# A six-stage decoder kernel: time-step chain in two halves, block-step rows, and the last steps of silu and gate on GpSimd

## The chip, the cores and the metric

The kernel runs on one core of a Trainium2 chip. The metric is the device time of one execution in microseconds (us). Five engines matter: TensorE (PE in the profile), VectorE (DVE), ScalarE (ACT), GpSimd (POOL) and SyncE (SP), which here only issues DMAs.

## The reference, cut to what matters

The reference runs six blocks over x of 4 x 256 tokens by 256 features, each with a layer norm in front and a residual behind. The kernel names them stages A to F: attention (A), hard-routed experts (B), a mixture of experts (C), a state-space block (D), attention without projections (E), a second mixture of experts (F). The change is in D and in the second half of C. D computes, with 64 heads of width 8, chunks of 128 tokens and 8 groups of state size 64:

```python
xBCzA = jnp.einsum('bld,ed->ble', input_, in_proj_w)
xBC, z, A_log = ...                       # 1536, 512 and 64 columns
xBC = silu(causal depthwise conv of 4 taps(xBC) + bias)
x, Bm, Cm = ...                           # 512, 512 and 512 columns
dt = jax.nn.softplus(A_log)
A_cum = jnp.cumsum(-dt within the chunk)
Lm = jnp.exp(segsum(A))                   # lower triangle: exp(A_cum[s] - A_cum[z]), above it 0
Y_diag = jnp.einsum('bcshn,bczhn,bhcsz,bczhp->bcshp', Cm, Bm, Lm, X)
states = jnp.einsum('bcshn,bhcs,bcshp->bchpn', Bm, exp(A_cum[-1] - A_cum), X)
Y_off = jnp.einsum('bcshn,bchpn,bhcs->bcshp', Cm, states before, exp(A_cum))
yf = Y_diag + Y_off + D * x / dt
out = jnp.einsum('bld,ed->ble', yf * jax.nn.silu(z + z_bias), out_proj_w)
```

## The kernel before, in words

`schedule` writes one list of steps (kind, stage, index) for the whole kernel, and every engine walks the same list and does its share of each step, so the list is the order of work on every engine. Semaphores carry the data dependences. PSUM banks are rings; `number` gives each use its place. Ring T is one bank, with a wait of PE for the read of the use before it.

**Stage C.** It goes over the tokens in two halves. A half has 13 tiles of hidden units (2 shared, 11 routed). For a tile j PE does 12 matmuls of 512 columns (L1374), ACT the silu, DVE two products (L1746, L1751), ACT and DVE split the result in two parts (L973, L1757), and PE multiplies tile j - 2 by the down weights (L1398). ACT and POOL split the weights of tile j + 2 (L961, L791). Beside the second half stand the first 8 channel pairs of D (`BESIDE_C`): projection on PE (din, din2: L1411, L1418), a copy to SBUF on ACT (ev: L996, L998), three conv taps on DVE (L1781), silu on ACT (L1007).

**Stage D before its loop.** When C has ended, DVE adds the residual (L1704) and normalises batches 2 and 3 (L1544 to L1555, with the power on POOL, L739). PE turns them (lt: L1168). Then comes the time-step chain for all 8 x 64 columns at once: projection (dt_in: L1433), a softplus that POOL, ACT and DVE hand to one another (L1013 to L1029, L817 to L827, L1807 to L1810), cumulative sums by a triangular matmul (acum: L1441), copies (L1033), a split in three bf16 parts (L1824 to L1833), a transpose for unit 0 (at: L1446), its copy (atc: L1044, L1045), and SP's DMAs that put the rows in the form that the loop wants (L711, L713). Channel pair 8 stands between.

**The loop of D.** Its 8 units are the (batch, chunk) pairs. A unit has 16 slots (`NHG`), one for each 4 heads; `LAG` and `MUL_LAG` say how many slots later the scan and the mul of a slot stand, and `UNIT_SLOTS` and `PAIR_SLOTS` the slots of all else. In a slot:

- ssd: PE writes a bank with a mask (a matmul of `maskt` with the identity, 0 or -1e30: L1482) and adds the differences of cumulative sums, a matmul with 15 contraction rows (L1484);
- exp: ACT writes exp of the bank to one of 8 buffers M (L1066);
- mul: DVE multiplies M by the C-B product in place (L1849), both inputs in SBUF;
- scan: PE multiplies with the spread x (L1136), after `m_ready`.

Around them, in a unit: the C-B products (cb: PE L1469, copied by DVE in cbc: L1839), the chunk states (L1494, L1504, yo: L1858), the projection and gate of z (dz, dz2, zt: L1798, zth on ACT: L1019, zsm: L1801), y_t, yfs (DVE: Du added L1875, Y_off added in odd units L1880, times the gate L1881), the output projection (L1512 to L1521, added to x by dx, L1885), xt and xtp (transposed x, spread and multiplied by POOL: L843 to L852). Three channel pairs stand beside each of units 0 to 4: L1411, L1418, L996, L998, the taps L1781, th (tanh) on ACT L1009 and silu on DVE L1791. `raw` has two buffers: ev of a pair waits for the silu of the pair two before it (`xs_ready`). The input of ring R (L1411) waits for the read of the use before.

The lines of the loop as they stand before:

```python
("ssd")  mm(bk[:, :], identb[:, :], maskt[:, :].unsqueeze(1).to_broadcast([P, HG, P]),
            start=True, stop=False, skip_group_check=True)
         mm(bk[:, :], rows_z[:, hg, :], rows_s[:, :, hg, :], start=False, stop=True,
            skip_group_check=True).then_inc(e_full, 1)
("mul")  v.tensor_tensor(m, m, CBs[:, u % 2, hg // (NV // NG):NG:NG // HG, :], ALU.mult).then_inc(m_ready, 1)
```

## Time and profile before

| | us |
|---|---|
| median of 3 runs | 995.91 (994.95 to 996.75) |
| the profiled execution: its time | 990.7 |
| its span | 988.9 |
| end of C's last matmul to the first ssd of D | 408.68 to 455.65 |
| loop of D (first cb to the last matmuls) | 456.7 to about 700 |

| engine | busy | of the span |
|---|---|---|
| PE | 810.5 | 82% |
| DVE | 577.0 | 58% |
| ACT | 383.7 | 39% |
| POOL | 216.6 | 22% |

The shares are means over six stages with different limits. The page's slices show PE at nine tenths and more from about 460 to 680 us, with DVE at seven to eight tenths, and both low around 420 to 450 us. The granted TensorE clock had a mean of 0.899 over the span.

### The profile page before, as it was taken

The page shows a single profiled execution, that of the slowest core. Times are in us where ns is not written, and L with a number is a line of the kernel's source. Part 1 is how long each engine was busy: PE and PEld are TensorE (multiplying, and loading weights), DVE is VectorE, ACT ScalarE, POOL GpSimd, SP SyncE. Part 2 cuts the span into 40 slices and gives each one's busy share as a digit, 9 for nine tenths or more (in the row PEclk, how much of TensorE's full clock was granted, in tenths as well). Part 3 has the DMA queues.
Part 4 walks back from the last instruction along what each step waited for, and adds up shares of the span by engine and source line. Part 5 has one row for each costly group of instructions (what it writes and reads, how often), then busy time and mean ns, then how long its engine had stood idle before and what let it go on. Part 6 is the DMA issues. An engine that isn't in the chain of part 4 may idle for free.

```text
span 988.9 us, 14763 instructions
## 1 busy us (share of the span) xinstructions
PE 810.5 (82%) x5680; PEld 523.6 (53%) x5680; DVE 577.0 (58%) x1188; ACT 383.7 (39%) x653; POOL 216.6 (22%) x210
## 2 busy tenths in 40 slices
PE   1577777599799799656999999998667786899998
PEld 0334443258677588533445444444445454677776
DVE  5666642544545457525878788568566653545443
ACT  1124334101444355233566465354124344444442
POOL 3200000223433322141101111011411201442432
PEclk9889979799999899866989899699778788899999
DMA  9000001001121211000000000000000001222331
GB/s 311 29 2 1 3 1 49 1 0 32 49 81 53 71 54 33 9 0 5 5 3 6 4 5 6 3 5 4 1 2 2 1 1 50 81 80 64 84 96 40
DMA packets 17831, 32.77 MB, mean 33 GB/s; under 512 B 5819, under 2 KB 9787, under 8 KB 17494
## 3 DMA queue, kind: packets, MB, share of 16 engines
q1 hardware_dynamic: 17762, 31.83, 10.4%
q8 instruction: 46, 0.75, 0.3%
q14 instruction: 23, 0.19, 0.1%
HBM read 29.85 MB, written 1.05 MB: 31 GB/s over the span
## 4 chain that ended last, share of the span: by engine, by line
PE 60%; DVE 20%; issue 9%; ACT 4%; POOL 4%; DMA 1%; SPq 1%; DVEq 0%; ACTq 0%; POOLq 0%
PE bank L1374 13%; PE bank L1398 8%; PE bank L1136 4%; PE bank L1484 3%; PE bank L1321 3%; PE bank L1482 3%; PE bank L1411 3%; PE bank L1418 2%; DVE s_xn L1555 2%; PE bank L1336 2%; DVE s_arena L1627 2%; PE bank L1265 2%; POOL s_rstd L739 1%; PE bank L1208 1%; PE bank L1384 1%
## 5 line engine op out<-in xcount | busy, mean ns | idle before, releaser
L791 POOL TENSOR_TENSOR s_wl<-s_wmoe,s_wh 128x768 fp32r<-128x768 f32 x54 | 99.2, 1839 | 175.0 <-ACT s_wh L961 175.0
L910 ACT ACTIVATE s_arena<-bank 128x512 f32<-128x512 f32 x96 | 56.6, 597 | 106.2 <-PE bank L1241 55.2
L1746 DVE TENSOR_TENSOR s_act<-bank,s_sg_moe 128x512 f32<-128x512 f32 x54 | 37.3, 691 | 82.4 <-PE bank L1374 75.8
L1627 DVE TENSOR_REDUCE s_arena<-bank 128x2 f32<-128x512 f32 (+1 forms) x96 | 64.6, 686 | 35.6 <-PE bank L1212 18.9
L1374 PE MATMUL bank<-s_xh,s_wh 128*128 128x512 f32 x216 | 73.1, 421 | 8.2 <-POOL s_wl L791 8.2
L973 ACT CAST s_ah<-s_act 128x512 fp32r<-128x512 f32 x54 | 33.6, 621 | 101.7 <-DVE s_act L1751 79.2
L1374 PE MATMUL bank<-s_xl,s_wh 128*128 128x512 f32 x216 | 69.3, 403 | 0.0
L1398 PE MATMUL bank<-s_wh,s_ah 128*128 128x256 f32 x216 | 66.5, 308 | 2.8 <-DVE s_al L1757 2.8
L1374 PE MATMUL bank<-s_xh,s_wl 128*128 128x512 f32 x216 | 68.4, 399 | 0.0
L1781 DVE SCALAR_TENSOR_TENSOR s_arena<-s_arena,s_convw 128x256 f32<-128x256 f32 x144 | 63.7, 483 | 0.6
L1398 PE MATMUL bank<-s_wl,s_ah 128*128 128x256 f32 x216 | 61.6, 285 | 0.0
L1398 PE MATMUL bank<-s_wh,s_al 128*128 128x256 f32 x216 | 61.5, 285 | 0.0
L1757 DVE TENSOR_TENSOR s_al<-s_act,s_ah 128x512 fp32r<-128x512 f32 x54 | 37.3, 691 | 40.3 <-ACT s_ah L973 40.2
L1066 ACT ACTIVATE s_arena<-bank 128x512 f32<-128x512 f32 x64 | 38.2, 597 | 50.1 <-PE bank L1484 50.1
L1482 PE MATMUL bank<-s_maskt,s_identb 128*128 128x512 bf16 x128 | 52.3, 408 | 5.1 <-DMA s_arena<-s_arena 4.3
L739 POOL TENSOR_TENSOR s_rstd<-s_ve,s_mhalf 128x2 f32<-128x2 f32 x24 | 16.6, 691 | 175.0 <-DVE s_ve L1547 174.7
L1849 DVE TENSOR_TENSOR s_arena<-s_arena 128x512 f32<-128x512 f32 x64 | 42.9, 685 | 15.9 <-ACT s_arena L1066 15.6
L1484 PE MATMUL bank<-s_arena 15*128 15x512 bf16 x128 | 51.9, 406 | 0.0
L1066 ACT ACTIVATE s_early<-bank 128x512 f32<-128x512 f32 x64 | 38.4, 601 | 30.2 <-PE bank L1484 29.9
L1398 PEld LDWEIGHTS bank<-s_wh,s_ah 128*128 128x128 f32 x216 | 41.4, 192 | 13.5 <-issue 8.2
L1374 PEld LDWEIGHTS bank<-s_xl,s_wh 128*128 128x128 f32 x216 | 42.5, 197 | 9.8
L1168 PE MATMUL bank<-s_ident,s_xn 128*128 128x128 f32 x80 | 15.5, 327 | 39.0 <-DVE s_xn L1555 36.9
(232 smaller groups left out, 1745.6 us busy)
## 6 DMA issues: line engine op xcount, KB each, us to landing
s_wmoe<-in_wF SPq DMA_DIRECT2D x28, 384.0 KB, 3.1
s_wmoe<-in_wC SPq DMA_DIRECT2D x26, 384.0 KB, 3.0
s_win<-in_win SPq DMA_DIRECT2D x1, 2112.0 KB, 10.4
s_x<-in_x SPq DMA_DIRECT2D x4, 256.0 KB, 3.5
s_early<-in_ctxT SPq DMA_DIRECT2D x1, 1024.0 KB, 9.5
s_ctxn<-in_ctx SPq DMA_DIRECT2D x1, 1024.0 KB, 12.3
s_arena<-s_arena SPq DMA_DIRECT2D x64, 6.0 KB
out_x<-s_x SPq DMA_DIRECT2D x4, 256.0 KB, 2.8
```

Of the source, the lines that this page charges most:

```text
L791: g.tensor_tensor(wl[:, w % NS_, :], wmoe[:, w % NW, :], wh[:, w % NS_, :], ALU.subtract).then_inc(wl_ready, 1)
L910: a.activation(PT[:, p % NPT, :], AR[n % 3][:, :], ACT.Exp).then_inc(a_read, 1)
L1066: a.activation(M[k % NM], S[k % 2][:, :], ACT.Exp).then_inc(e_read, 1)
L1136: ins = mm(bk[j * 32:(j + 1) * 32, quarter * P:(quarter + 1) * P], xsp[u % 2][:, quarter, h, j, :, :].rearrange("p q w -> p (q w)"), M[k % ...
L1374: ins = mm(G[2 * (n % 2) + half][:, :], a_[:, k, half, :], b_[:, k, toks], start=(p_ == 0), stop=(p_ == len(parts) - 1))
L1398: ins = mm(Y[t // NT][:, (t % NT) * D:(t % NT + 1) * D], a_[:, w % NA, t * P:(t + 1) * P], b_[:, w % NS_, 2 * KD * P:], start=(j == 0 and ...
L1482: mm(bk[:, :], identb[:, :], maskt[:, :].unsqueeze(1).to_broadcast([P, HG, P]), start=True, stop=False, skip_group_check=True)
L1484: mm(bk[:, :], rows_z[:, hg, :], rows_s[:, :, hg, :], start=False, stop=True, skip_group_check=True).then_inc(e_full, 1)
L1627: v.tensor_reduce(nM[:, q, h0:h0 + heads], V[n % 2][:, :].rearrange("p (h k) -> p h k", h=heads), AX.X, ALU.max, negate=True).then_inc(v_r ...
L1746: v.tensor_tensor(act_[:, w % 2, :], G[2 * (n % 2) + 1][:, :], sg_moe[:, n % 2, :], ALU.mult).then_inc(g_read, 1)
L1781: ins = v.scalar_tensor_tensor(o, raw[:, m % NRAW, h, KS - 1 - k:KS - 1 - k + L], convw[:, ct, KS - 1 - k:KS - k], o, ALU.mult, ALU.add)
L1849: v.tensor_tensor(m, m, CBs[:, u % 2, hg // (NV // NG):NG:NG // HG, :], ALU.mult).then_inc(m_ready, 1)
```

## The change

Five things change.

1. The time-step chain is cut in two halves of 4 units (256 columns). Its steps have names of their own (dt_in, dtc, dt_p1 to dt_p3, dt_a1 to dt_a3, dt_sum, acum, acumc, last, lastc, dec_in, dec_exp, ap_hi, ap_mid, ap_lo, ddt). The first half stands beside tiles 4 to 10 of C's second half (`BESIDE_C_STEPS`), the second in slots 21 to 44 of D's loop (`SECOND_STEPS`: units 1 and 2). The turns of batches 2 and 3 move into slots 2 and 3 of the loop (`LATER_TURNS`). Its scratch moves from the M buffers, yf and yo to the part of `early` that is free by then. The POOL memsets of the spread buffers stand in xtp of units 0 and 1.
2. The mask is no matmul any more. 15 further contraction rows (`blocks` times steps in `onehot`, 16 columns a block) put -1e30 above the blocks on the diagonal; within a block the entries above the diagonal stay, mul clamps them with `min 1.0`, and cbc multiplies the C-B product by the lower triangle, both as `scalar_tensor_tensor` on DVE. `onehot` grows from 12 to 27 rows of 16 KB, and one DMA (`blocks`, 15 rows of 4 KB) is new.
3. silu of D's pairs goes from one DVE instruction to two `tensor_tensor` on POOL (L840, L841 of the kernel after). The same for the gate of z, zsm (L844, L845).
4. yfs keeps its first add on DVE; the add of Y_off and the product with the gate become the POOL step yfp (L850, L852), in slot 8.
5. The first pair of the loop is number 8 instead of 9, and some slots move by one.

The diff, cut to its core (the bodies of the renamed chain steps are as before, over 256 columns instead of 512, and are left out):

```diff
-FIRST_PAIRS = 9
+FIRST_PAIRS = 8
...
-UNIT_SLOTS = ((0, "cb", 0), (3, "state", 0), (3, "at", 1), (6, "y_t", -1), (7, "dz", 1), (8, "dz2", 1), (9, "dy_t", -1),
-              (12, "dy", -1), (13, "dy2", -1), (14, "xt", 1), (15, "xt1", 1),
-              (4, "atc", 1), (5, "ysc", -1), (7, "stc", 0), (10, "yfc", -1), (11, "zth", 1), (15, "xtc", 1), (15, "xtp", 1),
+UNIT_SLOTS = ((0, "cb", 0), (3, "state", 0), (3, "at", 1), (6, "y_t", -1), (7, "dz", 1), (8, "dz2", 1), (10, "dy_t", -1),
+              (13, "dy", -1), (14, "dy2", -1), (14, "xt", 1), (15, "xt1", 1),
+              (4, "atc", 1), (5, "ysc", -1), (7, "stc", 0), (11, "yfc", -1), (11, "zth", 1), (15, "xtc", 1), (15, "xtp", 1),
               (16, "xt1c", 1),
-              (1, "cbc", 0), (4, "yo", 0), (7, "yfs", -1), (9, "zt", 1), (12, "zsm", 1), (14, "dx", -1))
+              (1, "cbc", 0), (4, "yo", 0), (7, "yfs", -1), (8, "yfp", -1), (9, "zt", 1), (12, "zsm", 1), (15, "dx", -1))
+LATER_TURNS = (2, 3)
+SECOND_STEPS = ((21, "dt_in"), (22, "dtc"), (23, "dt_p1"), (24, "dt_a1"), (25, "dt_p2"), (26, "dt_a2"), (27, "dt_p3"), (28, "dt_a3"),
+                (29, "dt_sum"), (33, "acum"), (34, "acumc"), (37, "last"), (38, "lastc"), (39, "dec_in"), (40, "dec_exp"),
+                (41, "ap_hi"), (42, "ap_mid"), (43, "ap_lo"), (44, "ddt"))
+BESIDE_C_STEPS = ((4, "dt_in"), (4, "dtc"), (4, "dt_p1"), (5, "dt_a1"), (5, "dt_p2"), (5, "dt_a2"), (6, "dt_p3"), (6, "dt_a3"),
+                  (6, "dt_sum"), (7, "acum"), (7, "acumc"), (8, "last"), (8, "lastc"), (8, "dec_in"), (9, "dec_exp"),
+                  (9, "ap_hi"), (9, "ap_mid"), (10, "ap_lo"), (10, "ddt"))
 PAIR_SLOTS = (((1, "din"), (2, "din2"), (3, "ev"), (5, 1), (6, 2), (8, 3), (9, "th"), (10, "silu")),
               ((4, "din"), (5, "din2"), (6, "ev"), (9, 1), (10, 2), (11, 3), (12, "th"), (13, "silu")),
               ((10, "din"), (11, "din2"), (12, "ev"), (13, 1), (14, 2), (15, 3), (16, "th"), (18, "silu")))
-RR = 3 + 3 * HG
+RL = 3 + 3 * HG
+STEPS = 16
+RR = RL + STEPS - 1
...
+                        steps.extend((kind, nxt, 0) for at_j, kind in BESIDE_C_STEPS if at_j == j)
...
-            if not beside_c:
-                steps.append(("d_init", s, 0))
-            while late:
-                turn(*late.pop(0))
-            steps.append(("dt_in", s, 0))
-            chain = ["dt", "acum", "at", "atc", "ddt"]
-            for m in range(beside_c, FIRST_PAIRS):
-                din(m)
-                if m > beside_c:
-                    silu(m - 1)
-                if m == beside_c:
-                    steps.extend((kind, s, 0) for kind in ("dz", "dz2", "zt"))
-                taps(m)
-                if chain:
-                    steps.append((chain.pop(0), s, 0))
-            silu(FIRST_PAIRS - 1)
-            steps.extend((kind, s, 0) for kind in chain)
-            steps.extend((kind, s, 0) for kind in ("zth", "zsm", "xt", "xtc", "xtp", "xt1", "xt1c"))
+            assert beside_c == FIRST_PAIRS
+            steps.extend((kind, s, 0) for kind in ("at", "atc", "xt", "xtc", "xtp", "xt1", "xt1c", "dz", "dz2", "zt", "zth", "zsm"))
             units = B * NT
             slots = {}
 
             def put(slot, kind, key):
                 slots.setdefault(slot, []).append((kind, s, key))
 
+            for slot, (stage, b) in zip(LATER_TURNS, late):
+                put(slot, "lt", b)
+            late.clear()
+            for slot, kind in SECOND_STEPS:
+                put(slot, kind, 1)
...
+                    sp.dma_start(rows_z[RL:RR, :, :], A["blocks"]).then_inc(hot_in, 16)
...
+                elif kind == "silu":
+                    b, j = i
+                    m = b * (CT // 2) + j
+                    if m < beside_c:
+                        continue
+                    pool.wait_ge(tanh_ready, m - beside_c + 1)
+                    half, th = xs[:, b % 2, 2 * j:2 * j + 2, :], raw[:, m % NRAW, :, KS - 1:]
+                    link(g.tensor_tensor(th, th, half, ALU.mult))
+                    g.tensor_tensor(half, th, half, ALU.add).then_inc(xs_ready, 1)
+                elif kind == "zsm":
+                    pool.wait_ge(z_tanh, i + 1)
+                    link(g.tensor_tensor(zs[:, i % 2, :], zs[:, i % 2, :], zt[:, :], ALU.mult))
+                    g.tensor_tensor(zs[:, i % 2, :], zs[:, i % 2, :], zt[:, :], ALU.add).then_inc(zs_ready, 1)
+                elif kind == "yfp":
+                    pool.wait_ge(v_read, at["V"]["y_t", s, i] + 1)
+                    if i % 2:
+                        pool.wait_ge(v_read, at["V"]["state", s, i, 1] + 1)
+                        link(g.tensor_tensor(yf, yf, yo, ALU.add))
+                    pool.wait_ge(zs_ready, i + 1)
+                    g.tensor_tensor(yf, yf, zs[:, i % 2, :], ALU.mult).then_inc(yf_ready, 1)
...
-                            pe.wait_ge(hot_in, 32)
+                            pe.wait_ge(hot_in, 48)
...
-                    mm(bk[:, :], identb[:, :], maskt[:, :].unsqueeze(1).to_broadcast([P, HG, P]),
-                       start=True, stop=False, skip_group_check=True)
-                    mm(bk[:, :], rows_z[:, hg, :], rows_s[:, :, hg, :], start=False, stop=True,
-                       skip_group_check=True).then_inc(e_full, 1)
+                    mm(bk[:, :], rows_z[:, hg, :], rows_s[:, :, hg, :], start=True, stop=True
+                       ).then_inc(e_full, 1)
...
-                        v.tensor_copy(CBs[:, i % 2, par:NG:2, :], V[n % 2][:, :].rearrange("p (g s) -> p g s", g=NG // 2)
-                                      ).then_inc(v_read, 1)
+                        v.scalar_tensor_tensor(CBs[:, i % 2, par:NG:2, :],
+                                               V[n % 2][:, :].rearrange("p (g s) -> p g s", g=NG // 2), -1.0,
+                                               tri[:, 0, :].unsqueeze(1).to_broadcast([P, NG // 2, P]),
+                                               ALU.mult, ALU.mult).then_inc(v_read, 1)
...
-                    v.tensor_tensor(m, m, CBs[:, u % 2, hg // (NV // NG):NG:NG // HG, :], ALU.mult).then_inc(m_ready, 1)
+                    v.scalar_tensor_tensor(m, m, 1.0, CBs[:, u % 2, hg // (NV // NG):NG:NG // HG, :], ALU.min, ALU.mult
+                                           ).then_inc(m_ready, 1)
...
-                    dve.wait_ge(v_read, n + 1)
-                    if c:
-                        dve.wait_ge(v_read, at["V"]["state", s, i, 1] + 1)
-                        link(v.tensor_tensor(yf, yf, yo, ALU.add))
-                    v.tensor_tensor(yf, yf, zs[:, c, :], ALU.mult).then_inc(yf_ready, 1)
...
-    arrays["onehot"] = np.tile(np.repeat(np.eye(HG), 3, 0)[:, :, None, None], (1, 1, NHG, P)).astype(bf)
+    onehot = np.tile(np.repeat(np.eye(HG), 3, 0)[:, :, None, None], (1, 1, NHG, P))
+    step = P // STEPS * np.arange(1, STEPS)
+    before = np.where(i[None, :] < step[:, None], NEG, 0.0)
+    inside = (i[None, :] // (P // STEPS) == np.arange(1, STEPS)[:, None]).astype(np.float64)
+    arrays["onehot"] = np.concatenate([onehot, np.tile(before[:, None, None, :], (1, HG, NHG, 1))], 0).astype(bf)
+    arrays["blocks"] = np.tile(inside[:, None, :], (1, NHG, 1)).astype(bf)
```

How the order of instructions changes is shown at three places; rows are those of the program before and after, each with its own line numbers.

On PE, between the last down matmul of C and the first ssd of D, before (L1433 is dt_in, L1441 acum, L1446 at, L1482 mask, L1484 ssd):

```order
756 L1168 MATMUL bank<-s_ident,s_xn 128x128 x8
757 L1433 MATMUL bank<-s_win,s_xnT 128x64 x16
758 L1411 MATMUL bank<-s_xnT,s_win 128x256 x2
759 L1418 MATMUL bank<-s_xnT,s_win 128x256 x2
760 L1423 MATMUL bank<-s_win,s_xnT 128x512
761 L1426 MATMUL bank<-s_win,s_xnT 128x512
762 L1441 MATMUL bank<-s_arena,s_tri 128x512 x2
763 L1446 MATMUL bank<-s_identb,s_arena 96x128 x2
764 L1455 MATMUL bank<-s_ident,s_arena 128x128 x4
765 L1460 MATMUL bank<-s_ident,s_arena 128x128 x4
766 L1482 MATMUL bank<-s_maskt,s_identb 128x512
767 L1484 MATMUL bank<-s_arena 128x512
```

and after, up to the turn of batch 2 (L1475 is at, L1511 ssd, L1196 the turns of batches 2 and 3):

```order
759 L1475 MATMUL bank<-s_identb,s_early 96x128 x2
760 L1484 MATMUL bank<-s_ident,s_arena 128x128 x4
761 L1489 MATMUL bank<-s_ident,s_arena 128x128 x4
762 L1451 MATMUL bank<-s_win,s_xnT 128x512
763 L1454 MATMUL bank<-s_win,s_xnT 128x512
764 L1511 MATMUL bank<-s_arena 128x512
765 L1498 MATMUL bank<-s_arena 128x128 x8
766 L1511 MATMUL bank<-s_arena 128x512
767 L1439 MATMUL bank<-s_xnT,s_win 128x256 x2
768 L1511 MATMUL bank<-s_arena 128x512
769 L1196 MATMUL bank<-s_ident,s_xn 128x128 x4
```

Between C and the first ssd, the turns, dt_in, acum and the pair are gone; the transpose of unit 0's rows comes first, and an ssd is one instruction instead of two.

On POOL, the work of about one unit with three pairs, before (L843, L845, L852 are xtp, L739 the norm's power):

```order
75 L843 COPY s_wmoe<-s_arena 128x4x4x8 x4
76 L845 TENSOR_TENSOR s_arena<-s_arena 128x512
77 L739 TENSOR_TENSOR s_rstd<-s_ve,s_mhalf 128x2
78 L843 COPY s_arena<-s_arena 128x4x4x8 x4
79 L845 TENSOR_TENSOR s_arena<-s_arena 128x512
```

and after (L840 and L841 silu, L844 and L845 zsm, L850 and L852 yfp, L867 and L869 xtp):

```order
113 L741 TENSOR_TENSOR s_rstd<-s_ve,s_mhalf 128x2
114 L840 TENSOR_TENSOR s_arena<-s_arena 128x2x256
115 L841 TENSOR_TENSOR s_arena<-s_arena 128x512
116 L852 TENSOR_TENSOR s_arena<-s_arena 128x512
117 L840 TENSOR_TENSOR s_arena<-s_arena 128x2x256
118 L841 TENSOR_TENSOR s_arena<-s_arena 128x512
119 L844 TENSOR_TENSOR s_arena<-s_arena 128x512
120 L845 TENSOR_TENSOR s_arena<-s_arena 128x512
121 L840 TENSOR_TENSOR s_arena<-s_arena 128x2x256
122 L841 TENSOR_TENSOR s_arena<-s_arena 128x512
123 L867 COPY s_arena<-s_arena 128x4x4x8 x4
124 L869 TENSOR_TENSOR s_arena<-s_arena,s_early 128x512
```

Nine or ten `tensor_tensor` instructions with both inputs in SBUF are new in a unit, in POOL's one queue.

On ACT, in tiles 5 and 6 of C's second half, after (L978 is the silu of a tile, L1049, L1052 and L1057 the three functions of the chain, L1031 the pairs' silu, L997 and L985 the splits); before, the stretch has none of the table loads and none of these three:

```order
127 L978 ACTIVATE s_sg_moe<-bank 128x512
128 L1049 ACT_TABLE_LOAD
129 L1049 ACTIVATE s_early<-s_early 128x256
130 L1052 ACT_TABLE_LOAD
131 L1052 ACTIVATE s_early<-s_early 128x256
132 L1020 ACTIVATE s_arena<-bank,s_convw 128x256 x2
133 L1022 COPY s_arena<-bank 128x2x256
134 L997 CAST s_ah<-s_act 128x512
135 L985 CAST s_wh<-s_wmoe 128x768
136 L978 ACT_TABLE_LOAD
137 L978 ACTIVATE s_sg_moe<-bank 128x512
138 L1057 ACT_TABLE_LOAD
```

In all there are 7 table loads beside C's second half, one at the start of D and two in its loop, where before there were three, all ahead of the loop.

## Rows read from the trace of the kernel before

**Rows 1.** Windows: busy us of each engine with counts, clock, DMA share, GB/s

```profile
408.70:455.65 46.95, 19.93 (x66) 13.64 (x67) 19.22 (x40) 13.54 (x21) 15.62 (x16) 0.62 0.03 6
456.70:616.00 159.30, 154.32 (x1208) 76.33 (x1207) 121.77 (x248) 91.22 (x176) 17.67 (x29) 0.93 0.02 4
616.00:700.00 84.00, 75.97 (x651) 33.44 (x651) 57.22 (x115) 35.16 (x64) 8.50 (x16) 0.86 0.02 4
520.40:552.00 31.60, 31.60 (x276) 16.32 (x273) 25.48 (x52) 19.52 (x38) 5.49 (x9) 1.00 0.02 5
```

**Rows 2.** Chain that ended last, from C's end to D's loop: start, us, what

```profile
408.70 1.28 DVE s_x L1704 x2
...
417.93 7.06 PE bank L1433 x32
...
429.44 1.28 ACT L1022
430.74 0.64 ACT s_arena L1022
...
449.07 0.43 PE bank L1446 x2
...
453.33 2.19 DMA s_arena<-s_arena
455.65 0.58 PE bank L1482
```

**Rows 3.** PE in order of time, a slot of unit 2 with a pair

```profile
528.45 0.38 PE L1482 MATMUL bank<-s_maskt,s_identb 128*128 128x512 bf16 x1
528.76 0.39 PE L1484 MATMUL bank<-s_arena 15*128 15x512 bf16 x1
529.07 0.43 PE L1136 MATMUL bank<-s_arena 128*32 128x128 f32 x8
529.43 1.13 PE L1418 MATMUL bank<-s_xnT,s_win 128*128 128x256 f32 x4
530.39 0.38 PE L1482 MATMUL bank<-s_maskt,s_identb 128*128 128x512 bf16 x1
```

**Rows 4.** SP's DMA issues ahead of unit 0

```profile
450.20 3.09 SPq L711 DMA_DIRECT2D s_arena<-s_arena  x4
453.33 0.81 SPq L713 DMA_DIRECT2D s_arena<-s_arena  x1
```

**Rows 5.** DMA issues of the page: count, KB each, us to landing

```profile
s_early<-in_ctxT SPq DMA_DIRECT2D x1, 1024.0 KB, 9.5
```

**Rows 6.** C beside D's pairs: a window of one tile

```profile
363.70:370.10 6.40, 6.40 (x34) 5.21 (x33) 4.62 (x9) 3.73 (x8) 1.82 (x2) 1.00 0.18 61
```

**Rows 7.** Lines in D: min/median/max ns, first and last start

```profile
L1441 PE MATMUL bank<-s_arena,s_tri x4: 1057/1140/1220, 440.3 to 444.1; 128*128 128x512 f32 x4
L1849 DVE TENSOR_TENSOR s_arena<-s_arena x64: 677/683/693, 460.1 to 689.8; 128x512 f32<-128x512 f32 x64
L1791 DVE SCALAR_TENSOR_TENSOR s_arena<-s_arena x16: 678/682/686, 440.2 to 618.4; 128x512 f32<-128x512 f32 x16
L1881 DVE TENSOR_TENSOR s_arena<-s_arena x8: 691/691/692, 504.2 to 697.2; 128x512 f32<-128x512 f32 x8
L1781 DVE SCALAR_TENSOR_TENSOR s_arena<-s_arena,s_convw x144: 471/479/829, 359.2 to 611.6; 128x256 f32<-128x256 f32 x144
L845 POOL TENSOR_TENSOR s_arena<-s_arena x8: 1067/1071/1509, 454.3 to 668.1; 128x512 f32<-128x512 f32 x8
```

**Rows 8.** Stage B, DVE and POOL products side by side: lines, then timeline

```profile
L1692 DVE TENSOR_TENSOR s_arena<-s_arena,s_early x6: 1211/1224/3147, 204.6 to 222.6; 128x1024 f32<-128x1024 f32 x6
L796 POOL TENSOR_TENSOR s_arena<-s_xnT,s_early x2: 2119/2156/2194, 179.0 to 183.6; 128x1024 f32<-128x1024 f32 x2
...
204.63 5.42 DVE L1692 TENSOR_TENSOR s_arena<-s_arena,s_early 128x1024 f32<-128x1024 f32 x3
204.68 3.16 POOL L803 TENSOR_TENSOR s_arena<-s_arena,s_early 128x1024 f32<-128x1024 f32 x1 [18.87 <-DVE s_arena L1689]
```

**Rows 9.** Window of the time-step chain's DVE part

```profile
438.00:452.90 14.90, 6.42 (x14) 2.62 (x14) 9.67 (x17) 4.54 (x9) 1.48 (x1) 0.50 0.00 1
```

154 lines of the change are left out of this document (80 added, 74 removed).

## The prediction

> **What bounds the kernel now.** I read the windows first. Between C's last matmul and D's first ssd stand 46.95 us in which PE is busy 19.93 us, at a mean clock of 0.62, and DVE 19.22 us: nobody is full there [rows 1]. The chain of waits says what it is, a string of dependent steps: residual and norm, the 32 small matmuls of dt_in (7.06 us), a table load and a function on ACT three times, the transpose, SP's issues and a landing, and then the ssd at 455.65 [rows 2]. In the loop it is another picture. Units 0 to 4 take 159.30 us with PE busy 154.32 and DVE 121.77; unit 2 alone has PE at 31.60 of 31.60 at full clock, DVE at 25.48 [rows 1]. So PE bounds the loop, and DVE stands only 20% below it. Units 5 to 7 with the hand-over to E take 84.00 us, PE 75.97, DVE 57.22 [rows 1]. A part of the change that frees PE is worth its time only down to where DVE is.
>
> **Part 1, the way into the loop.** After C's end the residual runs to 408.70 + 1.28 = 409.98 [rows 2], and stays. What is left in front of the first ssd is the transpose of unit 0's rows (its inputs were made beside C), atc, and the DMAs. From the transpose's start at 449.07 to SP's first issue at 450.20 pass 1.13 us, from there to the ssd 5.45 us [rows 2, 4]. That makes 409.98 + 1.13 + 5.45 = 416.6. SP issues one DMA more in front of these, so I take 417.5. The rows of `onehot` grow from 192 to 432 KB and now must land here, where they had 45 us before. A load of 1024 KB took 9.5 us to land [rows 5]; 432 KB lie below that, and by share it would be 4.0 us, so at 410.4 + 4.0 it is in time, and with all 9.5 us it would put the ssd at 420. The norms of batches 2 and 3 now run beside these DMAs on DVE; they reach 416 as before and cbc stands behind them, in time. Gain: 455.65 - 417.5 = 38 us (34 to 39).
>
> **Part 2, what C pays.** A tile beside a pair takes 6.40 us and PE is busy all of it, ACT 3.73, POOL 1.82, DVE 4.62 [rows 6]. PE gets 16 of the 32 small matmuls, half of 7.06 us at half clock [rows 2], so 1.8 us at full clock, and two triangular matmuls of half width: one instruction of 512 columns took 1.14 us at half clock and there were four [rows 7], so a quarter of 4.2 us, 1.0 us. Then PE's next projection waits three times (dt_in, acum, last) for a copy on ACT to give ring T's bank back, some 0.7 us each. Sum 5 us. ACT gets seven table loads, 429.44 to 430.74 each, 1.28 us [rows 2], three of them around tile 5: 3.9 us and three functions and a wait for POOL on top of 3.73 in a tile of 6.40. PE needs ACT's silu of a tile one tile and more later, so I cost that at nothing; without the cover it is the excess of tiles 5, 6 and 9 over 6.40, some 2 + 1 + 0, and the standing for POOL, up to 7 us. C pays 5 us (3 to 12).
>
> The Trainium skill speaks against this (ScalarE: Activation LUTs, What ACT_TABLE_LOAD costs): a load of 1283 ns is followed by a drain of about 1380, 2.66 us for a switch. The load agrees; the row shows no drain behind it, as the function starts at 430.74 [rows 2]. By the page the seven switches would cost 18.6 us of ACT instead of 9.0, and C's price would go toward its upper end.
>
> **Part 3, the mask.** An ssd's two matmuls start 0.31 us apart, and the scan starts 0.31 us after the second [rows 3]; their sum on PE per slot falls by 0.31 us, 16 slots by 8 units, 39.7 us. More contraction rows don't change the columns streamed. mul becomes a scalar_tensor_tensor: at 128x512 that form takes 682 ns (L1791) where the product takes 683 (L1849) [rows 7]; nothing. cbc reads one bank and a small tile instead of one bank: nothing, as it is bound by the same 512 columns.
>
> **Part 4, DVE against POOL.** DVE loses 15 silus, 7 gates and 12 instructions of yfs in the loop, 0.68 to 0.69 us each [rows 7]. In units 0 to 4 it is 15 + 5 + 6 = 26 by 0.68, 17.7 us. It gets the second half of the chain: the window with all of it shows DVE busy 9.67, less 0.68 for a silu, 9.0 [rows 9]; half the columns cost more than half of it, between 4.5 and 9.0; I take 5.5. Left 121.8 - 17.7 + 5.5 = 109.6 us.
>
> Now what POOL does beside it. In stage B DVE and POOL ran the same kind of product together. The DVE product alone takes 1.21 us, the one that met POOL 3.15; POOL's took 3.16 instead of 2.12 [rows 8]. In the timeline three DVE products and one of POOL lie in 204.63 to 210.05: 5.42 us, which is 3 x 1.21 + 2.12 less 0.3 [rows 8]. They ran one after the other, not beside each other. In D itself xtp's product has a maximum of 1509 against 1071 ns, as it waited for a DVE product, and a tap 829 against 479 [rows 7]. DVE's mul and taps, most of its time in the loop, have both inputs in SBUF; all that moves to POOL has too, and there it takes two instructions of 1.07 us [rows 7] for one of 0.68. A POOL instruction of 1.07 us keeps DVE out for some 0.92 us by the same reading (2.12 less 0.15 for its start). In units 0 to 4 POOL gets 30 for silu, 10 for zsm, 6 for yfp: 46 x 0.92 = 42 us, and three short ones of the chain, 1.5 us. DVE's time is then 109.6 + 43.8 = 153.4 us of 159.3. What was to relieve DVE loads it, 17.7 us out and 42 us in.
>
> The Trainium skill has the same as a rule (SBUF — State Buffer, Who interferes with whom): a DVE instruction with two SBUF inputs contends with a GpSimd instruction that reads SBUF, as an exclusive lock over the whole instruction. By that rule the change gives DVE a queue of POOL's instructions; without it DVE would have the 17.7 us as room, the first rival below.
>
> PE in units 0 to 4: 154.3 - 80 x 0.31 = 129.5, and 1.8 + 1.0 for the second half of the chain, 1 for the turns: 133.3. So DVE bounds, at 153.4 plus the jitter of two engines that need each other. I take 157, a gain of 2 (9 if a third of the exclusions fall where DVE would wait anyway, a loss of 13 if each row of waits is paid in full).
>
> **Part 5, units 5 to 7.** PE 76.0 - 48 x 0.31 = 61.1, with pair 23 (two projections of 0.96 us, 529.43 to 530.39 [rows 3]) 63.0. DVE 57.2 - 8 x 0.68 + 6 taps x 0.45 = 54.5, and 12 POOL instructions x 0.92, 65.5 of 84. Neither is full, and the end is a chain into E. I take 10 (3 to 15). The loop gives 12.
>
> **Sum.** 38 - 5 + 2 + 10 = 45 us. The profiled execution took 990.7 us (span 988.9); 990.7 - 45 = 945.7. The median of the runs shown, 995.91, lies 5.2 above it, and I add that: 951 us. All bounds at once, which is unlikely, would give 936 to 984; I take 940 to 968 as the forecast's own range.
>
> **Rivals.** First, the exclusion costs little: POOL's instructions fall into DVE's waits, and the loop follows PE. For it speaks that yfs, cbc, yo and zt read a bank and are not shut out; against it the 5.42 us. Then units 0 to 4 take 136 (-23) and the rest falls 15: 38 - 5 + 23 + 15 = 71, 925 us. Chance 17%.
>
> Second, C doesn't hide the first half: ACT stands behind loads and POOL, PE behind ACT for its bank, and C pays 15 to 25 us instead of 5: 961 to 971. For it speaks ACT's tile 5 at 3.73 + 3.9 + functions, over 6.40; against it that this comes in two or three tiles only. Chance 13%.
>
> Third, slower. ev of a pair waits on ACT for the silu two pairs before (`raw` has two buffers), and the exps stand behind it, then PE's two ssd banks. The silu's way grows from 0.68 us to two POOL instructions of up to 1.51 us, plus xtp's in front of one in three. If all of it shows, each pair costs 3.0 - 0.7 = 2.3, and the third one 3.5 more: 16 x 2.3 + 5 x 3.5 = 55 us, 45 of them used up by the gain: 1006. It decides from 2.8 us a pair; slot distances of two or more slots (2 us each) speak against it. Chance 6%.
>
> Fourth, the change doesn't start the loop early, as the first ssd waits for something left (`onehot` landing late, cbc behind the norms), 20 of the 38 us gone: about 970. Chance 4%.
>
> The forecast has 60%. Range: 925 to 972, which leaves out half of the first rival's chance and all of the third's. Faster by over 0.2% (2 us, what these measurements can tell): 0.93; within it 0.02; slower 0.05.
>
> **What would show it.** Right: the first ssd 8 to 10 us after C's last matmul; no mask rows; in units 1 to 3 PE with waits for DVE's mul and DVE near full, DVE's mul and taps with a mean well above 683 and 479 ns, POOL's added rows with a mean above 1.07 us; a unit with pairs at 30 to 33 us. Wrong: those means unchanged and a unit at 27 us (then about 925), C's second half longer by over 12 us, or ev waiting for POOL's silu in each unit by several us.

## The result, and the profile after

The kernel after takes 0.9875 of the time of the kernel before, interval 0.9841 to 0.9909: some 12.5 us of 994.95 (the median of before in that comparison). I had forecast some 44 us (951 us, with a range of 925 to 972), so the time lies outside it, and the sign alone is right. The ratio rests on the five undisturbed ones of twelve executions (the profiled one is among them), 979.05 to 987.89 us at a mean granted clock of 0.864 to 0.882; the other seven took 998.48 to 1013.95 at 0.837 to 0.861, and the median of all twelve, 998.92, is no better than before's 994.95.

| | before | after |
|---|---|---|
| profiled execution, span (us) | 990.7, 988.9 | 980.79, 979.0 |
| mean granted clock | 0.899 | 0.879 |
| end of C's last matmul to first ssd | 47.0 | 8.5 |
| first ssd to last dx | 248.0 | 263.8 |

From the page of the kernel after: the busy times, and the clock in 40 slices.

```profile
PE 797.0 (81%) x5556; PEld 520.3 (53%) x5556; DVE 603.3 (62%) x1167; ACT 391.9 (40%) x667; POOL 299.9 (31%) x276
PEclk9989988599899799978988888595878788899999
```

Windows of the kernel after, in the columns of [rows 1]: C's end to the first ssd, units 0 to 4, the rest of the loop with the hand-over, and a stretch in it.

```profile
421.60:430.05 8.45, 4.90 (x14) 2.73 (x15) 6.53 (x16) 1.82 (x4) 3.30 (x4) 0.66 0.28 70
430.05:602.05 172.00, 144.43 (x1110) 76.23 (x1110) 145.49 (x232) 95.09 (x185) 86.86 (x82) 0.85 0.02 4
603.20:694.00 90.80, 81.17 (x653) 38.34 (x649) 64.34 (x116) 37.89 (x70) 29.71 (x32) 0.72 0.02 4
611.90:635.80 23.90, 23.90 (x134) 9.38 (x127) 15.68 (x29) 9.57 (x18) 7.82 (x9) 0.51 0.01 3
```

The first row is the 46.95 us of [rows 1] shrunk to 8.45. The second holds units 0 to 4, from the first ssd to the first of unit 5: 172.0 us, where it took 156.1 before (455.65 to 611.74) and the forecast had it 2 us shorter than that. From there to the last dx it is 91.8 us, as before (91.9), where the forecast had it 10 shorter. In the last row PE is busy all of the time and gets half of its clock, the 1.2 GHz level.

The second thing forecast, that POOL's products keep DVE out, is there too. Lines of the kernel after (min/median/max ns, first and last start): DVE's taps and one of the two forms of mul, then the first of POOL's two products of silu and the second of the gate's (zsm).

```profile
L1808 DVE SCALAR_TENSOR_TENSOR s_arena<-s_arena,s_convw x144: 471/480/2061, 365.4 to 618.7; 128x256 f32<-128x256 f32 x144
L1871 DVE SCALAR_TENSOR_TENSOR s_arena<-s_arena x64: 675/684/1758, 434.5 to 678.5; 128x512 f32<-128x512 f32 x64
L840 POOL TENSOR_TENSOR s_arena<-s_arena x16: 1089/1269/1718, 448.7 to 620.4; 128x512 f32<-128x512 f32 x16
L845 POOL TENSOR_TENSOR s_arena<-s_arena x8: 1265/1598/1599, 434.3 to 651.3; 128x512 f32<-128x512 f32 x8
```

The medians of DVE's lines are those of [rows 7]: most DVE instructions take what they took, and some wait for POOL. The longest mul went from 693 to 1758 ns, the longest tap of the loop from 565 to 1493, and 26 of its 96 taps take over 600 where none did. (The 2061 is a tap beside C, at 406.6, which POOL's new products don't reach.) Over the loop the mean of a tap goes from 481 ns to 708, of a mul from 689 to 804. In order of time, two meetings: DVE's rows first, then POOL's.

```profile
480.02 2.02 DVE L1808 SCALAR_TENSOR_TENSOR s_arena<-s_arena,s_convw 128x256 f32<-128x256 f32 x2
482.57 0.68 DVE L1816 SCALAR_TENSOR_TENSOR s_arena<-bank,s_zb 128x512 f32<-128x512 f32 x1
483.17 2.59 DVE L1808 SCALAR_TENSOR_TENSOR s_arena<-s_arena,s_convw 128x256 f32<-128x256 f32 x2
```

```profile
479.42 1.82 POOL L852 TENSOR_TENSOR s_arena<-s_arena 128x512 f32<-128x512 f32 x1
482.79 1.27 POOL L840 TENSOR_TENSOR s_arena<-s_arena 128x512 f32<-128x512 f32 x1 [0.57 <-ACT s_arena L1033]
484.14 1.33 POOL L841 TENSOR_TENSOR s_arena<-s_arena 128x512 f32<-128x512 f32 x1
```

A pair of taps takes 2.0 and 2.6 us where two medians make 0.96; the instruction with one input in a bank, at 482.57, keeps its 0.68. What waits for DVE then, from the waits of the kernel after in 430 to 603 (us, times, longest): ACT's tanh for the taps, and PE's ssd for ACT's exp.

```profile
ACT s_arena L1033 <- DVE s_arena L1808: 28.3, 11, 6.5
PEld bank L1511 <- ACT s_early L1094: 24.1, 6, 6.0
PE bank L1511 <- ACT s_early L1094: 21.9, 5, 5.7
```

Before, the first of these was 4.4 us.

### The profile page after: what moved, and what is told of

Same layout as the page of the kernel before. It is cut to its first block, busy times and chain, and to the rows that moved or that the text cites. A ratio compares the mean times of both kernels' runs of the same rounds, so it can differ in the third digit from the quotient of the medians.

```text
span 979.0 us, 14586 instructions
## 1 busy us (share of the span) xinstructions
PE 797.0 (81%) x5556; PEld 520.3 (53%) x5556; DVE 603.3 (62%) x1167; ACT 391.9 (40%) x667; POOL 299.9 (31%) x276
## 4 chain that ended last, share of the span: by engine, by line
PE 29%; DVE 16%; issue 8%; ACT 3%; POOL 2%; DMA 0%; DVEq 0%; ACTq 0%; SPq 0%; POOLq 0%
PE bank L1402 7%; DVE s_arena L1808 5%; PE bank L1426 4%; PE bank L1164 3%; PE bank L1511 3%; PE bank L1439 1%; DVE s_early L1871 1%; PE bank L1446 1%; DVE s_arena L1871 1%; PE bank L1548 1%; DVE s_arena L1654 1%; PE bank L1293 1%; PE bank L1498 1%; DVE s_xn L1582 1%; POOL s_rstd L741 1%
## 5 line engine op out<-in xcount | busy, mean ns | idle before, releaser
L1808 DVE SCALAR_TENSOR_TENSOR s_arena<-s_arena,s_convw 128x256 f32<-128x256 f32 x144 | 87.0, 644 | 3.3 <-ACT s_arena L1022 2.6
L1511 PE MATMUL bank<-s_arena 30*128 30x512 bf16 x128 | 57.3, 448 | 25.1 <-ACT s_early L1094 21.9
L997 ACT CAST s_ah<-s_act 128x512 fp32r<-128x512 f32 x54 | 33.6, 622 | 101.8 <-DVE s_act L1778 79.5
L1784 DVE TENSOR_TENSOR s_al<-s_act,s_ah 128x512 fp32r<-128x512 f32 x54 | 37.4, 692 | 38.7 <-ACT s_ah L997 38.5
L1871 DVE SCALAR_TENSOR_TENSOR s_arena<-s_arena 128x512 f32<-128x512 f32 x64 | 53.9, 872 | 9.1 <-ACT s_arena L1094 8.8
L1511 PEld LDWEIGHTS bank<-s_arena 30*128 30x128 bf16 x128 | 11.9, 93 | 70.3 <-issue 35.1
L1402 PEld LDWEIGHTS bank<-s_xh,s_wh 128*128 128x128 f32 x216 | 39.7, 200 | 15.4 <-DVE s_act L1773 7.2
L1871 DVE SCALAR_TENSOR_TENSOR s_early<-s_early,s_arena 128x512 f32<-128x512 f32 x64 | 46.4, 737 | 2.4 <-ACT s_early L1094 2.2
```

Source lines behind the costliest of these rows:

```text
L997: a.copy(ah[:, w % NA, :], act_[:, w % 2, :]).then_inc(ah_ready, 1)
L1402: ins = mm(G[2 * (n % 2) + half][:, :], a_[:, k, half, :], b_[:, k, toks], start=(p_ == 0), stop=(p_ == len(parts) - 1))
L1511: mm(bk[:, :], rows_z[:, hg, :], rows_s[:, :, hg, :], start=True, stop=True).then_inc(e_full, 1)
L1784: v.tensor_tensor(al[:, w % NA, :], act_[:, w % 2, :], ah[:, w % NA, :], ALU.subtract).then_inc(al_ready, 1)
L1808: ins = v.scalar_tensor_tensor(o, raw[:, m % NRAW, h, KS - 1 - k:KS - 1 - k + L], convw[:, ct, KS - 1 - k:KS - k], o, ALU.mult, ALU.add)
L1871: v.scalar_tensor_tensor(m, m, 1.0, CBs[:, u % 2, hg // (NV // NG):NG:NG // HG, :], ALU.min, ALU.mult).then_inc(m_ready, 1)
```

## The experiments

Two disputes were to be settled: what POOL's products cost in time (not in DVE's busy time), and whether the half clock of some stretches has to do with the mask matmul that is gone. "Ballast" below means the old mask matmul issued ahead of an ssd into the same bank, where the ssd then overwrites it: PE's old work, with no part in the result. Ratios are to the kernel before, run beside it on the same chip.

### Without POOL: e1_all_dve, e2_silu_dve

e1 is the kernel after with silu, zsm and the end of yfs as the kernel before has them; e2 takes back silu alone. The part that both share, cut to its core:

```diff
-                    pool.wait_ge(tanh_ready, m - beside_c + 1)
-                    link(g.tensor_tensor(th, th, half, ALU.mult))
-                    g.tensor_tensor(half, th, half, ALU.add).then_inc(xs_ready, 1)
...
+                    dve.wait_ge(tanh_ready, m - beside_c + 1)
+                    v.scalar_tensor_tensor(half, raw[:, m % NRAW, :, KS - 1:], 1.0, half, ALU.add, ALU.mult
+                                           ).then_inc(xs_ready, 1)
```

> The kernel after, with silu, the gate of z and the two last steps of yfs back on DVE; chain in halves and block rows stay. Exclusion theory (POOL's products keep DVE out, DVE's lateness is what the loop of D pays for): taps and mul go back to about 0.44 and 0.68 us a piece, no wait of PE for ACT of 5 us in the loop, units 0 to 4 fall from 34 to about 27 us and the time from about 982 to 940. Queue theory (th and ev stand in ACT's queue in front of the exps, whoever does the silu): DVE is as full as before, ACT's waits for taps stay at 20 us and more in the loop, 965 to 980. Clock theory (the loop is long because PE is granted half clock after gaps that the early start makes): no large change, 975 or more.

> The kernel after, with only silu back on DVE; the gate and the last steps of yfs stay on POOL. Exclusion theory: 32 of the 60 moved POOL products go, so rather more than half of the gain of the run with all on DVE, 955 to 965. Latency theory (what hurts is that ev waits for a silu that takes two POOL instructions): nearly all of the gain, within 3 us of the run with all on DVE.

e1: 0.9631 [0.9592, 0.9671]. e2: 0.9791 [0.9746, 0.9836]. A tap of e1 takes 481 ns in the mean, as before; of e2 624. So the POOL part makes the kernel slower. But e1 isn't where the first rival stood (925), nor at the 940 expected of it: it took 957.3 and 959.3 us, on which the ratio rests, and 979.7 and 983.2. e2, 970.0 to 980.5 us, lies above both of its ranges. e1's window of units 0 to 4, and a stretch in it:

```profile
427.60:584.70 157.10, 147.04 (x1109) 77.00 (x1109) 124.78 (x254) 95.33 (x185) 24.46 (x35) 0.84 0.02 4
513.60:551.10 37.50, 37.21 (x191) 18.12 (x191) 25.56 (x59) 15.10 (x29) 3.28 (x6) 0.50 0.01 3
```

PE is busy 147 us where I had worked out 133, at a mean clock of 0.84; 37.5 us in one piece are at half clock, with PE at 37.21 busy.

### Reads or the way through POOL: e3_write_only; the order: e4_th_later

```diff
-                    link(g.tensor_tensor(th, th, half, ALU.mult))
-                    g.tensor_tensor(half, th, half, ALU.add).then_inc(xs_ready, 1)
+                    for n in range(3):
+                        link(g.memset(th, 0.0))
+                    g.memset(half, 0.0).then_inc(xs_ready, 1)
```

> The kernel after, with the two POOL products of each silu in the loop of D replaced by four memsets of the same tiles (some 0.5 us each by the 1.80 us that a memset of 128x2048 took), so that POOL is busy as long and the silu is ready as late, but POOL reads nothing from SBUF; the silu of those pairs is left out of the computation. Exclusion theory: taps and mul beside these instructions take 0.44 and 0.68 us again, the time is near that of the run with only silu on DVE, 950 to 965. Latency theory: as the kernel after, about 982.

> The kernel after, with tanh and silu of each pair one or two slots later in the list (and the third pair one slot later), so that ACT reaches the tanh when DVE has done the taps. Exclusion theory: DVE stays as full, the time falls by 0 to 8 us. Queue theory: ACT's 28 us of waits for taps go and the time falls by 12 to 20 us, to about 965.

e3 leaves the silu of these pairs out. 0.9806 [0.9748, 0.9865], taps 611 ns: like e2, not like after, though the interval touches after's and the times (968.1 to 981.4 us) lie between its two ranges. It is repeated below with ballast. e4 has the tanh and silu of the first two pairs one or two slots later and all of the third pair one or two; one of its three lines:

```diff
-              ((4, "din"), (5, "din2"), (6, "ev"), (9, 1), (10, 2), (11, 3), (12, "th"), (13, "silu")),
+              ((4, "din"), (5, "din2"), (6, "ev"), (9, 1), (10, 2), (11, 3), (14, "th"), (15, "silu")),
```

0.9956 [0.9906, 1.0006]. ACT's wait for the taps (in 430 to 603 us, as above) went from 28.3 us to this, and the time didn't fall:

```profile
ACT s_arena L1033 <- DVE s_arena L1808: 12.4, 6, 3.7
```

The idea that ACT's queue behind the tanh is what makes the loop long gets no support: it wanted 12 to 20 us. The granted clock of the profiled execution is lower too, 0.863 against 0.879, so this run alone doesn't rule it out.

### The clock: e5_filler, e6_filler_after

e5 is e1 with ballast ahead of each ssd, e6 the kernel after with it.

```diff
+                    mm(bk[:, 0:4 * P], identb[:, :], maskt[:, :].unsqueeze(1).to_broadcast([P, 4, P]), start=True, stop=True)
                     mm(bk[:, :], rows_z[:, hg, :], rows_s[:, :, hg, :], start=True, stop=True
```

> The kernel with everything back on DVE (chain in halves, block rows), and in front of each ssd the old mask matmul once more as pure ballast: the ssd's rows overwrite its result. Clock theory (without the mask PE has gaps, is granted half clock in long stretches of D's loop, 37.5 us in one stretch of the run without ballast, and gives back there what the mask cost): the half-clock stretches in the loop shrink, and the time is no more than that without ballast, 957, though PE has 40 us more to do. Work theory (PE's work counts as in the kernel before, at full clock): 20 to 35 us slower, 980 to 990.

> The kernel after with the same ballast matmul in front of each ssd. Clock theory: fewer half-clock stretches in the loop and the same time or less, 970 to 985, with little spread between runs. Work theory: PE gets 40 us more beside a DVE that is nearly full, 990 to 1005.

e5: 0.9638 [0.9615, 0.9662], four executions within 961.43 and 965.47 us. e6: 0.9824 [0.9801, 0.9847], 979.98 to 984.34. With the 39.7 us of PE work (by my estimate) put back, neither is measurably slower than its kernel without it (0.9631 and 0.9875), and the spread is gone. Units 0 to 4 and then the rest of the loop, of e5:

```profile
428.10:582.10 154.00, 147.83 (x1191) 75.81 (x1191) 126.42 (x258) 96.92 (x186) 24.82 (x38) 0.98 0.02 4
582.10:673.80 91.70, 87.08 (x711) 40.34 (x710) 62.87 (x128) 38.84 (x71) 10.44 (x19) 0.82 0.02 4
```

and of e6:

```profile
430.80:605.90 175.10, 159.39 (x1190) 80.57 (x1190) 145.52 (x232) 97.22 (x186) 87.06 (x85) 0.90 0.02 4
605.90:697.70 91.80, 85.65 (x711) 40.06 (x711) 66.38 (x118) 38.87 (x72) 31.21 (x34) 0.83 0.02 4
```

Two readings. With 80 mask matmuls more, e5's units 0 to 4 hold PE 147.83 us, e1's 147.04: what the mask's removal takes off PE, the lower clock (0.84 against 0.98) puts back. And e6 against e5, on one chip, is POOL's price beside the ballast: 1.9% or 20.6 us by the medians (983.2 against 962.6), 21.1 us in these five units and nothing behind them. The ballast doesn't hold the clock fully beside POOL: 0.90 against 0.98. Of the 21.1 us PE is busy for 11.6 (159.39 against 147.83, with the same matmuls) and stands still for 9.5. So the price has two halves, waits of PE and work of PE at a lower clock. That the waits bring the clock down is my reading; no run separates the two.

### The two halves of the change alone: e7_rows_only, e8_pool_only, e9_rows_ballast

e7 is the kernel before with the block rows in place of the mask matmul, e8 the kernel before with silu, gate and yfs on POOL, e9 is e7 with ballast. The heart of e7's edit:

```diff
-                    mm(bk[:, :], identb[:, :], maskt[:, :].unsqueeze(1).to_broadcast([P, HG, P]),
-                       start=True, stop=False, skip_group_check=True)
-                    mm(bk[:, :], rows_z[:, hg, :], rows_s[:, :, hg, :], start=False, stop=True,
-                       skip_group_check=True).then_inc(e_full, 1)
+                    mm(bk[:, :], rows_z[:, hg, :], rows_s[:, :, hg, :], start=True, stop=True
+                       ).then_inc(e_full, 1)
```

> The kernel before with the block rows alone: no mask matmul, mul with min, cbc with the triangle; chain, silu and gate as before. Work theory: PE bounds D's loop, 128 x 0.31 us = 39.7 us go, the time falls by 25 to 35 us to 960 to 970. Clock theory: the loop gains much less, as half-clock stretches come in, 5 to 15 us, 980 to 990, with more spread than the kernel before.

> The kernel before with silu, the gate and the last steps of yfs on POOL alone; the mask and the chain as before. Exclusion theory: taps and mul beside POOL's products take 0.6 to 0.7 and 0.8 us, D's loop grows by 10 to 25 us and the time with it, 1005 to 1020. If DVE's room is enough: 993 to 998.

> The kernel before with the block rows, and the mask matmul kept in front of each ssd as ballast. Clock theory: the 92 us and the other half-clock stretches of the run with block rows alone go, and the time comes back from 1020 to that of the kernel before, within 5 us. If the block rows themselves were slow (the product with min, cbc with the triangle, 30 contraction rows): it stays near 1020 or goes above it.

e7: 1.0216 [1.0195, 1.0238]; taking 39.7 us of work (by my estimate) off the busiest engine made the kernel slower, which neither of its two ranges had. (One execution of 3649.73 us is left out of it; I don't know its cause.) e8: 1.0394 [1.0369, 1.0418], beyond the 1020 expected: POOL's products cost 39 us here, nearly twice the 20.6 of e6 against e5. Its units 0 to 4 begin at 458.2 and end at 642.1 us, 183.8 us at this clock:

```profile
456.70:640.00 183.30, 165.23 (x1149) 80.58 (x1150) 135.89 (x211) 87.75 (x170) 77.43 (x71) 0.84 0.02 4
```

PE is busy 165 us there, where it was 154.32 in 159.30 us before at 0.93 [rows 1]: here too a part of the price is clock. So the prices of the parts can't simply be added.

e9: 1.0004 [0.9984, 1.0025], ten executions: the block rows, the `min` and the triangle cost nothing by themselves. e5 differs from e9 by the chain in halves and the slots that go with it: 0.9638 against 1.0004, some 36 us. That is what the early start is worth alone; the mask's removal and POOL's products together leave 12 of it. A stretch of e7, then two ssds of it with what stands between them:

```profile
629.60:721.80 92.20, 90.96 (x591) 39.61 (x592) 53.78 (x109) 34.07 (x61) 8.49 (x16) 0.50 0.01 3
```

```profile
661.11 0.60 PE L1485 MATMUL bank<-s_arena 30*128 30x512 bf16 x1
661.65 0.66 PE L1139 MATMUL bank<-s_early,s_wmoe 128*32 128x128 f32 x8
662.24 0.60 PE L1485 MATMUL bank<-s_arena 30*128 30x512 bf16 x1
```

92 us at half clock, with PE busy 90.96. From an ssd to the scan behind it pass 0.54 us, where [rows 3] have 0.31.

### What kind of ballast: e10_thin_ballast, e11_ballast_0_5, e15_half_0_5

```diff
-                    mm(bk[:, 0:4 * P], identb[:, :], maskt[:, :].unsqueeze(1).to_broadcast([P, 4, P]), start=True, stop=True)
+                    mm(bk[:, :], identb[0:16, :], maskt[0:16, :].unsqueeze(1).to_broadcast([16, HG, P]), start=True, stop=True)
```

That is e10, the same 512 columns with 16 contraction rows in place of 128. e11 is e5 with `if u <= 5:` ahead of the ballast, e15 is e11 with 256 columns in place of 512.

> All on DVE, with ballast of the same 512 columns and the same time on PE, but of 16 contraction rows instead of 128. If the clock follows how long PE is busy: as with the full ballast, 961 to 965 in all runs, no long half-clock stretch in units 0 to 4. If it follows how much of the array works: as without ballast or worse, runs of 957 to 990 and long half-clock stretches, now with 40 us more for PE to do.

> All on DVE with the full ballast, but only in units 0 to 5. Clock theory: units 0 to 4 stay at full clock as with the full ballast; units 6 and 7, which took 23.0 and about 43 us with it and 19.2 and 37 without, give 4 to 9 us back: 953 to 959. Work theory: 12 us less than with the full ballast at best.

> All on DVE, ballast of half the columns (128 rows, 256 columns, some 0.2 us) in units 0 to 5. If the clock is held by this too: 6 x 16 x 0.1 = 10 us of PE less, and where PE is the later one it shows, 943 to 950. If half is too little: half-clock stretches in units 0 to 4 in some runs, 950 to 975 with a spread like the run without ballast.

e10 took 1022.43 to 1069.81 us (before 993.45 beside it), the slowest kernel of all by the median (1062.31), and beyond the 957 to 990 expected. A stretch of it, and a piece in order of time:

```profile
551.00:643.10 92.10, 92.10 (x438) 38.25 (x436) 50.08 (x102) 32.97 (x62) 7.34 (x12) 0.50 0.01 3
```

```profile
560.35 0.60 PE L1491 MATMUL bank<-s_maskt,s_identb 16*128 16x512 bf16 x1
560.76 0.63 PE L1492 MATMUL bank<-s_arena 30*128 30x512 bf16 x1
561.32 0.66 PE L1144 MATMUL bank<-s_early,s_arena 128*32 128x128 f32 x8
```

The same three instructions of e5, with 128 rows in the first:

```profile
500.06 0.38 PE L1491 MATMUL bank<-s_maskt,s_identb 128*128 128x512 bf16 x1
500.37 0.38 PE L1492 MATMUL bank<-s_arena 30*128 30x512 bf16 x1
500.69 0.43 PE L1144 MATMUL bank<-s_arena 128*32 128x128 f32 x8
```

e15 took 956.79 us once and 977.62 to 981.89 three times (no ratio is worked out for it; before 995.38): with half of the ballast the time isn't held, and the profiled execution (981.89) has long stretches at half clock in units 0 to 4 again, as its slices show:

```profile
PEclk9889898799899899978579569995878788899999
```

e11 is the fastest kernel of the study, 0.9593 [0.9554, 0.9632], 950.13 to 956.68 us; it beats both kernels. Its units 0 to 4 and the rest:

```profile
427.40:581.40 154.00, 147.84 (x1191) 75.80 (x1190) 126.40 (x258) 96.55 (x186) 24.83 (x37) 0.98 0.02 4
581.40:662.40 81.00, 74.36 (x679) 36.24 (x679) 62.80 (x129) 38.72 (x72) 10.81 (x21) 0.86 0.02 5
```

In units 6 and 7 leaving the mask out is worth what it should be: 81.00 us against e5's 91.70, where 32 slots by 0.31 us make 9.9. Why the clock doesn't pay for it there isn't shown.

### C, and silu beside the ballast: e12_c_light, e13_silu_dve_ballast, e14_write_only_ballast

e12 is e11 with acum and last one tile later and ddt behind the last tile:

```diff
-                  (6, "dt_sum"), (7, "acum"), (7, "acumc"), (8, "last"), (8, "lastc"), (8, "dec_in"), (9, "dec_exp"),
-                  (9, "ap_hi"), (9, "ap_mid"), (10, "ap_lo"), (10, "ddt"))
+                  (6, "dt_sum"), (8, "acum"), (8, "acumc"), (9, "last"), (9, "lastc"), (9, "dec_in"), (10, "dec_exp"),
+                  (10, "ap_hi"), (10, "ap_mid"), (11, "ap_lo"), (13, "ddt"))
```

> As the run with ballast in units 0 to 5, and beside C's second half the cumulative sums one tile later and the reciprocal (ddt) behind the last tile. If PE's standing for acum's input (3.1 us in its tile) and DVE's lateness in C's last tiles (2.3 us) are what C pays beyond its matmuls: C's second half is 3 to 5 us shorter, 950 to 955. If not: the same as that run.

0.9586 [0.9559, 0.9613], the same as e11, by three of five executions (951.43 to 952.13 us). The other two took 967.79 and 968.58: in the profiled one of these, units 0 to 4 last 169.8 us for e11's 154.0, with a stretch of 30.7 us at half clock from 456.9 us on, although all of their ballast is there. So the ballast makes such stretches rarer; it doesn't rule them out. C's second half, from its first matmul to its last, got 1.5 us shorter, 93.3 for 94.8, not 3 to 5.

e13 is e2 with ballast, e14 is e3 with ballast; e14 too leaves the silu of those pairs out.

> The kernel after with silu back on DVE, gate and yfs on POOL, and the full ballast. Exclusion theory: of the 20.6 us between 983.2 (all on POOL) and 962.6 (all on DVE), both with ballast, about half stays, 970 to 975, with taps between 0.49 and 0.72 us. Latency theory: 962 to 966, as silu is the one that is waited for.

> The kernel after with the full ballast, and the two POOL products of each silu in D's loop replaced by four memsets of the same tiles (POOL busy as long or longer, silu ready as late, nothing read; the silu of those pairs is left out). Exclusion theory: as the run with silu on DVE and ballast, within 4 us, and the taps as short as there. Latency theory: as the kernel after with ballast, 980 to 985.

0.9826 [0.9795, 0.9857] and 0.9806 [0.9775, 0.9836]. The taps in units 0 to 4 (busy us, mean ns, idle before) of e6 with all on POOL, of e13 with silu on DVE, of e14 with silu's place taken by writes alone, and of e5 with all on DVE:

```profile
L1809 DVE SCALAR_TENSOR_TENSOR s_arena<-s_arena,s_convw 128x256 f32<-128x256 f32 x90 | 62.0, 729 | 2.7 <-ACT s_arena L1022 2.6
```

```profile
L1800 DVE SCALAR_TENSOR_TENSOR s_arena<-s_arena,s_convw 128x256 f32<-128x256 f32 x92 | 53.8, 624 | 0.8 <-ACT s_arena L1013 0.8
```

```profile
L1810 DVE SCALAR_TENSOR_TENSOR s_arena<-s_arena,s_convw 128x256 f32<-128x256 f32 x92 | 54.1, 628 | 1.8 <-ACT s_arena L1023 1.8
```

```profile
L1789 DVE SCALAR_TENSOR_TENSOR s_arena<-s_arena,s_convw 128x256 f32<-128x256 f32 x96 | 43.1, 492 | 0.0
```

POOL instructions that only write leave the taps as if they weren't there (628 against 624 ns); those that read make them 729. That agrees with the rule of the Trainium skill (SBUF — State Buffer, Who interferes with whom) that a DVE instruction with two SBUF inputs contends with a GpSimd one that reads, not with one that only writes. For the time, the windows of units 0 to 4 in the profiled executions, of e13 (its fastest, 970.11 us) and then e14:

```profile
430.30:596.10 165.80, 153.62 (x1201) 78.02 (x1202) 136.39 (x246) 96.98 (x187) 49.47 (x55) 0.94 0.02 4
427.90:595.50 167.60, 158.54 (x1191) 80.34 (x1190) 128.05 (x232) 97.43 (x186) 79.37 (x111) 0.91 0.02 4
```

By these windows e5 takes 154.0 us, e13 165.8 with gate and yfs on POOL, e6 175.1 with silu there too: some 12 us for the first two and 9 for silu. e14, with silu as late as on POOL but nothing read, is within 2 us of e13, so it isn't the lateness of silu that costs. By the whole time silu's share is smaller, between nothing (e13's ratio is e6's) and 7 us (their medians, on two chips). How the 20.6 us divide is known no better than that.

## Why the prediction was wrong, step by step

Two steps failed. Part 3 took 39.7 us off PE at an unchanged clock. Part 4 set units 0 to 4 to the larger of DVE's and PE's sums. Between the profiled executions (spans 988.9 and 979.0), by the first ssd of a unit (before, by the mask matmul in front of it):

| part | forecast | measured |
|---|---|---|
| ahead of C's second half | 0 | +3.9 |
| C's second half | +5 | +9.0 |
| C's end to the first ssd | -38 | -38.5 |
| units 0 to 4 | -2 | +15.9 |
| unit 5 to the last dx | -10 | -0.1 |
| sum | -45 | -9.8 |

**Part 1 was right** to half a microsecond. The ssd at 430.05 didn't wait for `onehot` or for cbc; its weight load waited 2.6 us, which the profile puts down to the constants of `blocks`, and the matmul 1.8 us for the rows' own DMA.

**Part 2 had the mechanism, not the size.** 9.0 us instead of 5, within 3 to 12. The windows of the same part of C's second half, before and after, are at clocks of 1.00 and 0.99, so this is not the clock:

```profile
339.30:408.70 69.40, 66.88 (x359) 54.34 (x358) 43.01 (x81) 35.10 (x64) 16.60 (x9) 1.00 0.11 36
343.20:421.60 78.40, 70.90 (x379) 57.20 (x378) 49.64 (x96) 47.23 (x78) 21.40 (x15) 0.99 0.11 32
```

Three of PE's rows in it:

```profile
378.98 0.67 PE L1470 MATMUL bank<-s_early,s_tri 128*128 128x256 f32 x2 [0.86 <-ACT s_arena L1022]
380.94 1.10 PE L1439 MATMUL bank<-s_xnT,s_win 128*128 128x256 f32 x4 [1.29 <-issue]
419.43 0.39 PE L1426 MATMUL bank<-s_wh,s_ah 128*128 128x256 f32 x1 [2.93 <-DVE s_al L1784]
```

The sums of PE's waits, with the one for al (a split that DVE makes) after and then before:

```profile
PE bank L1426 <- DVE s_al L1784: 3.2, 2, 2.9
PE bank L1439 <- issue: 2.3, 3, 1.3
PE bank L1470 <- ACT s_arena L1022: 0.9, 1, 0.9
PE bank L1398 <- DVE s_al L1757: 1.4, 1, 1.4
```

That accounts for the 9.0 us: PE's busy time grew by 4.0 (I had 2.8), the waits at the turns of ring T's bank came to 3.2 (I had three of 0.7), if the three put down to `issue` are such, and the waits for al grew by 1.8 (not in my sum). The table loads didn't reach PE. Behind a load stands its function at once:

```profile
363.88 1.28 ACT L1049 ACT_TABLE_LOAD   x1
365.18 0.42 ACT L1049 ACTIVATE s_early<-s_early 128x256 f32<-128x256 f32 x1
```

so the longer switch that the Trainium skill gives (ScalarE: Activation LUTs, What ACT_TABLE_LOAD costs) isn't seen in this trace either.

**Part 3 failed.** I wrote that PE's sum falls by 0.31 us a slot, "16 slots by 8 units, 39.7 us", and carried it into "PE in units 0 to 4 ... 133.3" and into the 10 us of part 5. The matmuls did go; PE's time didn't: it was busy 144.43 us in units 0 to 4, and in e1, without POOL in the way, 147.04. The mask is the one matmul of a slot with all 128 rows and 128 columns of the array; what is left between the projections are mostly the ssd with 30 rows and scans with 32 output columns. In such stretches the granted clock was at the 1.2 GHz level for 24 us (after), 37 (e1) and 92 (e7), with PE busy nearly throughout; in the 92 us of e7 these two kinds hold 58 of PE's 91 busy us, the rest are matmuls of more rows and columns. e7 shows it alone (the mask gone: 1.0216), e9 its reverse (back as ballast: 1.0004); e10 has the ballast's columns and a busy PE, and the clock falls all the same. That is shown; why the chip grants less for such work is not.

How much of the miss this is can only be estimated. From the first ssd to the last dx, by the windows' clock (twice the missing share), the time at half clock went from some 50 us in 248 to some 102 in 264. Among the five executions of after from 979 to 988 us the time rises by some 25 us for each 100 us more at half clock, over all twelve (to 1014 us at a mean clock of 0.837) by some 35. At these rates the 52 us more are 13 to 18 us of the 35 that the sum was short. The +3.9 ahead of C, in stages that the change leaves alone, may be the same: the granted clock from 0 to 240 us was 0.89 after and 0.91 before.

The Trainium skill (TensorE: Matmul & The Clock Gate, Part 1: The HAM clock gate) says that the throttle is the default and that a busy PE lifts it. By that alone e7 and e10 would run at 2.4 GHz in those 92 us. They were granted 0.50; the measurement decides.

I had read a clock of 0.93 in [rows 1] as a property of the stage. It was a property of the work that the change removed.

**Part 4 had the exclusion right and added it wrongly.** DVE without POOL would be busy 126.4 less the 17.7 us moved, 108.7 (I had 109.6); it was busy 145.5, so POOL's products took 37 us of DVE, where I had 43.8. But I set the units to the larger of DVE's 153.4 and PE's 133.3. In e5, with PE at 147.83 of 154.00 and DVE at 126.42, DVE had 27 us to spare, and still e6 took 21.1 us more. Forecast to be 2 us shorter than before, the units came out 15.9 longer, with neither engine full: PE busy 144.43 of 172.00, DVE 145.49. The waits shown above are the way that I see: a meeting delays an instruction that a tanh or an exp, and then PE, waits for, and room elsewhere on DVE doesn't take that back. With half of the 21.1 us as work of PE at a lower clock, this accounts for the other half at most.

**Part 5.** Its 10 us exist: from unit 5's first ssd to the last dx e11 takes 81.6 us, where the kernel before took 91.9. e1, with no ballast anywhere, takes 85.3, and the kernel after 91.8 at a clock of 0.72, which I take to be what uses them up.

**The rivals.** The first (exclusion costs little) fell: e5 against e6. The second (C) was right in direction, too small to decide. The third (ev behind POOL's silu) isn't seen: e14, with silu as late but nothing read, is as fast as e13. The fourth didn't happen. None of them had the clock in it, and that was the gap in the list.

That the sign came out right says little for the forecast: the 38 us of part 1 carried it, against two steps that went the other way.

What stays open: why half of the ballast's columns isn't enough, and why the full one fails in some executions (e12); how POOL's price divides between waits and clock, and between silu, gate and yfs; and why that price is 39 us in the kernel before. No ballast was tried that does useful work.

## What to carry to other kernels

Before taking a matmul off TensorE, look at what is left between the full ones. If these are matmuls of few rows or few columns, price the removal at either clock level, and try the kernel with the old matmul as ballast to see which part of a result is clock. A product with two SBUF inputs moved from VectorE to GpSimd isn't relief as long as VectorE's own instructions have two SBUF inputs; measure it by VectorE's mean against its median. When two engines hand work to each other each few microseconds, delays on one add to the other's time; the larger of two sums is only a lower bound. When a change has several parts, price each alone: here the early start gives 36 us and the other two parts take back 24.

## What the runs showed of the hardware that I had not expected

- The clock can be granted at half for 92 us with PE busy 90.96 of 92.20 (e7) and 92.10 of 92.10 (e10), on a mix in which matmuls of 16 or 30 contraction rows and ones of 32 output columns hold more than half of PE's time.
- 128 matmuls of 128 rows by 512 columns, whose results nobody uses, leave the time as it is or better (e9 1.0004 for e7's 1.0216) and narrow it: 961 to 965 us (e5) where the same kernel without them took 957 to 983 (e1). In units 0 to 5 alone they didn't always hold (e12: 951 to 952 us, and twice 968).
- The same 128 matmuls with 16 rows make it slower than none, 1062 us in the median.
- POOL memsets of 128x512 beside DVE's taps cost them nothing (628 against 624 ns), where POOL's products make them 729.
